# Attention over 16 heads: v and k^T v computed as G = x^T k and G Wv, with the gate's bias carried by a constant column of x

## The reference

```python
h = einsum('bhid,oi,od->bho', x, weighted_sum, weight)     # x (4,512,256,4)
h = concatenate([h, txt], axis=1)                          # (4,1024,256)
n = layernorm(h)                                           # no scale, no shift
q = elu(n @ Wq) + 1;  k = elu(n @ Wk) + 1                  # W* (256,1024): 16 heads of 64
v = n @ Wv;           g = sigmoid(n @ Wg + bg)
kv = einsum('bhnd,bhne->bhde', k, v);  k_sum = k.sum(axis=-2)
z = 1 / clip(einsum('bhnd,bhd->bhn', q, k_sum), 1e-6)
out = einsum('bhnd,bhde->bhne', q * 64**-0.5, kv) * z * g
h = h + out @ Wo
h = h + ffn(layernorm(h))                                  # two layers, not touched
```

## Time and profile before

| | us |
|---|---|
| median of 3 runs | 2147.8 (2147.47 to 2151.69) |
| the profiled execution | 2146.89 |
| its span, first to last instruction | 2145.1 |
| PE busy | 1979.4 (92%) |
| DVE busy | 1547.7 (72%) |
| ACT busy | 1088.3 (51%) |
| POOL busy | 435.6 (20%) |
| mean granted clock of PE | 0.969 |

### The profile page before, as it was taken

One profiled execution on the slowest core, in us unless ns is written; L12 is line 12 of the kernel. 1 busy time (PEld: TensorE's weight loads), 2 busy tenths in 40 slices (PEclk: granted clock), 3 DMA queues, 4 the chain that ended last, 5 costly groups with the idle time before them and its releaser, 6 DMA issues. The chain is left out here.

```text
span 2145.1 us, 42708 instructions
## 1 busy us (share of the span) xinstructions
PE 1979.4 (92%) x13792; PEld 1692.4 (79%) x13792; DVE 1547.7 (72%) x4590; ACT 1088.3 (51%) x2517; POOL 435.6 (20%) x265
## 2 busy tenths in 40 slices
PE   8799999899999959999999879995999999959998
PEld 8688788788878847888888668884888888857887
DVE  7356546546636668999998677775899999957777
ACT  5322232232222228888888624443777777743433
POOL 3100000000000014444444200002444444420010
PEclk9899999999999979999999989997999999989999
DMA  8000000000000020000000010001000000000002
GB/s 300 1 1 1 2 1 1 2 1 1 1 2 1 1 105 5 5 5 5 5 5 5 5 61 11 15 5 65 6 5 5 5 5 5 5 16 15 11 10 83
DMA packets 43179, 42.20 MB, mean 20 GB/s; under 512 B 8552, under 2 KB 37959, under 8 KB 43080
## 3 DMA queue, kind: packets, MB, share of 16 engines
q1 hardware_dynamic: 43080, 40.90, 5.8%
HBM read 32.49 MB, written 8.39 MB: 19 GB/s over the span
## 5 line engine op out<-in xcount | busy, mean ns | idle before, releaser
L908 ACT ACTIVATE l_probs<-l_probs,l_negmax 128x256 f32<-128x256 f32 x512 | 253.2, 496 | 65.1 <-DVE l_negmax L989 65.1
L116 PE MATMUL ps<-local_w_hi,l_xT 128*128 128x512 f32 x384 | 167.9, 437 | 37.1 <-DVE l_xT L982 31.2
L862 POOL TENSOR_TENSOR l_t<-l_t,l_t 128x1024 f32<-128x1024 f32 x64 | 152.9, 2388 | 196.3 <-DVE l_t L1035 196.3
L116 PE MATMUL ps<-attn_w_hi,attn_xT_hi 128*128 128x512 f32 x392 | 169.3, 432 | 18.5 <-issue 10.0
L866 POOL TENSOR_TENSOR l_t<-l_t,l_rnorm 128x1024 f32<-128x1024 f32 x64 | 121.9, 1905 | 307.9 <-DVE l_rnorm L1006 307.9
L419 ACT ACTIVATE attn_exp<-ps 128x512 f32<-128x512 f32 x130 | 77.6, 598 | 209.9 <-PE ps L118 209.9
L914 ACT ACTIVATE l_probsT<-ps 128x512 f32<-128x512 f32 x256 | 138.3, 594 | 49.5 <-PE ps L1133 49.5
L117 PE MATMUL ps<-attn_w_lo,attn_xT_hi 128*128 128x512 f32 x392 | 158.5, 404 | 0.0
L118 PE MATMUL ps<-attn_w_hi,attn_xT_lo 128*128 128x512 f32 x392 | 158.0, 403 | 0.0
L510 DVE TENSOR_SCALAR attn_exp<-attn_exp 128x512 f32<-128x512 f32 x130 | 58.8, 453 | 136.6 <-ACT attn_exp L419 136.5
L118 PE MATMUL ps<-local_w_hi,l_xT 128*128 128x512 f32 x384 | 155.4, 405 | 0.0
(11 more groups left out here) (210 smaller groups left out, 5832.2 us busy)
## 6 DMA issues: line engine op xcount, KB each, us to landing
tok_x<-x SPq DMA_DIRECT2D x16, 512.0 KB, 5.6
m_shifted<-shifted SPq DMA_DIRECT2D x20, 256.0 KB, 2.7
shifted<-x SPq DMA_DIRECT2D x64, 64.0 KB, 1.5
out<-x SPq DMA_DIRECT2D x8, 512.0 KB, 4.4
ffn_w_raw<-ffn_w SPq DMA_DIRECT2D x6, 640.0 KB
local_w_raw<-ffn_wqkv SPq DMA_DIRECT2D x4, 768.0 KB, 5.3
h<-txt SPq DMA_DIRECT2D x4, 512.0 KB, 9.6
attn_w_raw<-attn_Wk SPq DMA_DIRECT2D x1, 1024.0 KB, 7.5
```

Source lines behind the costliest of these rows:

```text
L116: nc.tensor.matmul(out, wh, mh, start=start, stop=False, skip_group_check=True)
L862: nc.gpsimd.tensor_tensor(t1[:], t1[:], t2[:], ALU.add).then_inc(s.summed.sem, 1)
L908: last = nc.scalar.activation(v, v, ACT.Exp, bias=nb[:, h:h + 1], scale=-1.0, accum_out=rsum[:, h:h + 1])
```

## The change

- **G in place of v.** kv = k^T v = k^T (x Wv) = (x^T k)^T Wv. In the key stage PE computes G = x^T k (256 x 1024, banks 2 to 5, summed over the tiles of a batch) instead of v; both sides are split, so these are 12 matmuls of 512 columns a tile. ACT splits off k's high part (`key_high`), DVE its low part (`key_low`), likewise for the normalised x as it stands (`xnh`, `xnl`). Once a batch ACT copies G to SBUF (`take_g`, 4 copies) and PE computes G Wv in f32 (`kv_products`, 16 pairs of instructions, moving Wv with a column of zeros or ones).
- **Constant column.** One column of x, number 128, is redundant, since the normalised columns sum to zero: row 128 of every weight is subtracted from all other rows on the chip (`load_base`, `subtract_base`: two more broadcast loads of 512 KB and two POOL subtractions a weight), and the column holds 1. The row that is freed carries the gate's bias, zero for the others. The bias matmuls, their rows and the DVE steps for them are gone. `normalise` becomes two instructions.
- **Where weights are made.** Only Wk is split, and only Wk and Wv shifted, in the token mixer. Wq, Wg (shift on POOL, high part on ACT, low part on POOL) and Wo are done in the key stage of batch 0.
- **Batches.** Batch 0 and batch 3 are written out, `Fori(1, B - 1)` covers 1 and 2. The first batch transposes its tiles between the keys. The last two tiles of a batch pass through the output product during the next batch's key stage; the last batch does without a next one and ends with them alone. `norm.finish` moves from the end of the key stage into u = 0, behind the copies of k^T v.

```diff
             for n in range(JT * B):
                 if n + 2 < JT * B:
                     x_hi(n + 2)
...
                 take(n)
+                if n in (5, 6):
+                    K.high_part(act, s, 0, n - 5)
...
         def _(pool):
-            nc.gpsimd.memset(K.zrow[:], 0.0).then_inc(s.zeroed.sem, 1)
-            nc.gpsimd.memset(ones[:], 1.0)
-            nc.gpsimd.memset(vs[:, :, :, P:VC], 1.0)
+            K.subtract_base(pool, s, 2)
+            K.low_part(pool, s, 2)
+            nc.gpsimd.tensor_copy(wv[:, 1, :, P:VC], K.ident[:, 0:1].unsqueeze(1).to_broadcast([P, PAIRS, 1]))
             nc.gpsimd.memset(kv[:], 0.0).then_inc(s.attn_set.sem, 1)
+            K.subtract_base(pool, s, 3)
+            K.low_part(pool, s, 3)
             pool.wait_ge(*s.attn_wo_hi.after(1))
             nc.gpsimd.tensor_tensor(wol[:], woraw[:], f32(woh[:]), ALU.subtract).then_inc(s.attn_wo_lo.sem, 1)
...
+            def take_g(b):
+
+                act.wait_ge(*s.attn_g_mm.after(TB * b + TB))
+                for half in range(2):
+                    for c in range(KC):
+                        nc.scalar.activation(gt[:, c, half * HALF:(half + 1) * HALF], ps[:, 2 + 2 * c + half],
+                                             ACT.Copy).then_inc(s.attn_gt.sem, 1)
...
+                for j in range(TB):
+                    key_features(b, j)
+                    if first:
+                        if j + 2 < TB:
+                            low(b, j + 2)
+                        if j + 3 < TB:
+                            normalise(b, j + 3)
...
+                    key_low(b, j)
...
-            def kv_products(b, j):
-                pe.wait_ge(*s.attn_feat.after(AB * b + 2 * j + 2))
-                pe.wait_ge(*s.attn_b_done.after(AB * b + 2 * j + 2))
+            def g_products(b, j):
+                pe.wait_ge(*s.attn_klo.after(2 * TB * b + 2 * j + 2))
+                if j == 0:
+                    pe.wait_ge(*s.attn_b_done.after(GB * b))
+                    pe.wait_ge(*s.attn_o.after(OB * b))
+                for c in range(KC):
+                    x = slice(c * P, (c + 1) * P)
+                    for half in range(2):
+                        cols = slice(half * HALF, (half + 1) * HALF)
+                        last = matmul3(nc, ps[:, 2 + 2 * c + half], xnh[:, j, x], xnl[:, j, x],
+                                       kh[:, j % 2, cols], kl[:, j % 2, cols], j == 0, j == TB - 1)
+                last.then_inc(s.attn_g_mm.sem, 1)
+
+            def kv_products(b):
+                pe.wait_ge(*s.attn_gt.after(4 * b + 4))
                 for g, (m0, m1) in enumerate(GROUPS):
                     for m in range(m0, m1):
...
+                        for c in range(KC):
+                            last = nc.tensor.matmul(ps[:, KV_BANKS[g], (m - m0) * VC:(m - m0 + 1) * VC],
+                                                    gt[:, c, m * P:(m + 1) * P], wv[:, c, m, :],
+                                                    start=(c == 0), stop=(c == KC - 1))
...
                 for j in range(TB):
+                    if first and j + 2 < TB:
+                        xt(b, j + 2)
+                    if not first and j == 1:
+                        out_transposes(b - 1, False, STAGES, 1)
+                    if not first and j in (2, 3):
+                        xt(b, j + 4)
                     if j < TB - 1:
                         keys(b, j + 1)
...
+                    if not first and j < 2:
+                        out_products(b - 1, False, STAGES, j)
+                    g_products(b, j)
...
+        def subtract_base(pool, s, k):
+            pool.wait_ge(*s.attn_w[k % 2].after(16 * KC * (k // 2 + 1)))
+            pool.wait_ge(*s.base_in.after(32 * (k + 1) + 16))
+            for c in range(KC):
+                raw = K.attn_raw[k][0][c]
+                row = K.attn_base[:, c].rearrange("p (m n) -> p m n", n=P) if k == 1 else K.attn_base[:, c]
+                last = nc.gpsimd.tensor_tensor(raw, raw, row, ALU.subtract)
+            last.then_inc(s.based.sem, 1)
```

More of the change, by code:

```diff
@@ L528, in residual, with h_stats @@
                                         ALU.add).then_inc(s.attn_t_done.sem, 1)
+            def h_stats(b, last, u):
+                dve.wait_ge(*s.attn_t_done.after(fills(b, last)[0](u, 5) + 1))
+                for w in range(2):
+                    tile = bass.ds(TB * b + 2 * u - 2 + w, 1)
+                    nc.vector.bn_stats(K.h_stats[:, tile], H[:, tile])
             def gated(b, n, *groups):
@@ L614, in _, with xt @@
+            STEADY = 2 * TB + 1 + 4 * STAGES + STATS_STEPS + 3 * len(GROUPS) * TB
+            batches(dve, counting)
+            for which in range(2):
+                ot_lo(B - 1, True, STAGES, which)
+                residual(B - 1, True, STAGES, which)
+            h_stats(B - 1, True, STAGES)
         @block.tensor
         def _(pe):
-            def xt(bank, xn_n, slot, fill_n):
-                pe.wait_ge(*s.attn_xn.after(xn_n + 1))
-                pe.wait_ge(*s.attn_t_done.room(fill_n, 2))
+            def xt(b, j):
+                n = xt_fill(b, j)
+                pe.wait_ge(*s.attn_xn.after(TB * b + j + 1))
+                pe.wait_ge(*s.attn_t_done.room(n, 2))
@@ L619, in xt, with rows @@
                 for c in range(KC):
-                    last = nc.tensor.transpose(ps[:, bank, c * P:(c + 1) * P], xn[:, slot, c * P:(c + 1) * P], K.ident[:])
+                    last = nc.tensor.transpose(ps[:, 6 + j % 2, c * P:(c + 1) * P], xn[:, j % 2, c * P:(c + 1) * P],
+                                               K.ident[:])
                 last.then_inc(s.attn_t_full.sem, 1)
-            def rows(w, tile, bank0, full, free, count, bias, halves=(0, 1)):
+            def rows(w, tile, bank0, full, free, count, halves=(0, 1)):
@@ L706, in _, with batch @@
-            pe.wait_ge(*s.attn_set.after(1))
-            with pe.Fori(0, B) as b:
-                for j in range(TB):
+                done.then_inc(s.attn_t_full.sem, 1)
+            def batch(b, first, last):
+                if first:
+                    xt(b, 0)
+                    xt(b, 1)
+                keys(b, 0)
+                if not first:
+                    out_transposes(b - 1, False, STAGES, 0)
+                for j in range(TB):
+                    if first and j + 2 < TB:
+                        xt(b, j + 2)
+                    if not first and j == 1:
+                        out_transposes(b - 1, False, STAGES, 1)
+                    if not first and j in (2, 3):
+                        xt(b, j + 4)
```

564 lines of the change are left out of this document (305 added, 259 removed).

## The result

| | before | after |
|---|---|---|
| median of the timed runs, us | 2148.8 (2147.47 to 2151.69) | 2126.0 (2122.05 to 2127.21) |
| the profiled execution / its span | 2146.89 / 2145.1 | 2122.05 / 2120.3 |
| PE busy, DVE busy, POOL busy | 1979.4, 1547.7, 435.6 | 1900.5, 1589.2, 449.2 |
| ratio, 95% interval | | 0.9889 (0.9872 to 0.9906) |

By the ratio the change saves 24 us, 1.1% (22.8 between the medians). The forecast was 2073.6 with a range of 2050 to 2092: the sign was right, two thirds of the gain were missing, and the range did not hold the time.

What follows compares the result with a forecast made beforehand. The prediction took PE's instruction list plus PE's waits to bound the attention. Its terms for mixer and attention summed to 691.2 against 765.4, -74.2 us, giving 2073.6 with a range of 2050 to 2092.

Steps and rivals of the forecast that it cites:

- DMA: 1 MB more ahead of x tiles 2 and 3: Token mixer: the added loads come ahead of x tiles that were 2 us early, later ones 10; no cost summed.
- DVE's steps in the mixer: Token mixer: layernorm steps of tile 9 get stuck beside POOL, tile 10 is 4.5 us late; bounds 0 and 7.
- Batch 0's keys: Batch 0's key stage: DVE stands behind POOL's instructions; first query after 74 us, bounds 54 and 80.
- Bias: Query stages: dropping the bias matmuls saves 0.48 us each, 7.7 a batch, bounds 5 to 8.
- Start of the query stage: Query stage: late norm.finish delays the first gating; 3.0 us of idle PE against 2.05, bounds 2 and 5.
- Key stages of batches 1 to 3: Keys, G, moved output products, transposes and waits take 54.3 us a batch, bounds 53 and 58.
- rival B: Key stages: the key chain becomes the bound; partly, 2092, chance 0.09; slower than before, over 2148, chance 0.02.
- Jumps: Attention loop: three jumps back become one, costing 5.2 us in idle time and slow matmuls; loop entry and exit cost nothing.
- rival C: Loop entry and exit: written-out code costs as a jump does there, +10.4 us, 2084; chance 0.08.
- End: Attention's end: the last two tiles run alone, 14.5 us with a lower clock, bounds 12.5 and 18.
- Rival A: Batch 0's keys and mixer: PE doesn't pay for DVE standing behind POOL; 20 us less, 2053; chance 0.17.
- Rival D: Key stages: compiled order or reused semaphores serialise G with k; chance 0.02.

Runs made afterwards that it cites:

- e1: The kernel after with the constant column's base row loaded over 128 partitions, not 127, and row 0 zeroed afterwards: 2086.2 us, ratio 0.9704.
- e2: The kernel after with the base rows read from a DRAM array holding all 128 copies, still over 127 partitions: 2130.3 us.
- e3: The kernel before with one extra load over 127 partitions into memory that nothing reads: 2173.3 us.
- e4: The kernel before with one extra load over 128 partitions into memory that nothing reads: 2148.8 us.
- e7: e1 with POOL's work beside batch 0's keys made short, most of Wq's and Wg's shift and three low parts left out: 2072.5 us, ratio 0.9645.
- e9: The kernel before without the 64 bf16 matmuls that add the gate's bias: 2124.6 us, ratio 0.9876.
- e10: The kernel before with k^T v cut to one of 8 pairs for tiles 0 to 6 of a batch: 2112.4 us, ratio 0.9829.
- e5: e1 with norm.finish moved to the end of the key stage: 2082.0 us, ratio 0.9693.
- e12: e1 with norm.finish at the key stage's end, all batches written out and POOL's subtractions in quarters: 2067.9 us, ratio 0.9621.
- e11: e1 with POOL's subtractions beside batch 0's keys in quarters, Wo's in eighths: 2078.7 us, ratio 0.9666.

## Why the prediction was wrong, point by point

The predicted span was 2145.1 - 74.2 = 2070.9, the kernel after has 2120.3, e1 2082.5.

| term | sum | after | e1 |
|---|---|---|---|
| token mixer, to the attention's start | 64.4 | 100.6 (+36.2) | 66.1 (+1.7) |
| batch 0's keys | 74.3 | 73.5 (-0.8) | 70.8 (-3.5) |
| first query of batch 0 to that of batch 3 | 448.0 | 458.8 (+10.8) | 460.2 (+12.2) |
| rest | 1484.2 | 1487.4 (+3.2) | 1485.3 (+1.1) |

- **The step that failed: "DMA: 1 MB more ahead of x tiles 2 and 3, which were 2 us ahead of their use; later tiles are 10 us ahead."** It priced the loads by volume and so put them at nothing. One of the two was a load over 127 partitions, which ran on one engine of 16 with x tiles behind it in the queue, and PE stood 20.7 and 17.1 us. The mixer's term of +4.5, bounds 0 and 7, was +40.7; with 128 partitions (e1) it was +6.2. e1 to e4 show the cause. The diff had the `P - 1`; I read it as 4 KB less. The bound was drawn from what was already in the queue, so it could not hold a load of a kind that the kernel before doesn't have.
- *DVE's steps in the mixer* were right: in e1, without the slow loads, the mixer grew by 6.2 where 4.5 was summed. Two steps of the layernorm's statistics, with 8 and 16 columns, got stuck beside POOL's two subtractions of 39.81 to 44.14, one behind each, and PE waited 3.42 us for a later tile, as walked through from the earlier trace rows. The rest is a stretch at the lower clock behind that wait, and the 1.33 that PE waited because of the loads' volume, for which the sum had nothing. DVE's timeline of e1:

```profile
40.05 1.99 DVE L151 TENSOR_SCALAR attn_mean<-attn_rstd 128x8 f32<-128x8 f32 x1
42.07 2.10 DVE L152 TENSOR_TENSOR attn_dev<-attn_stats,attn_mean 128x16 f32<-128x16 f32 x1
```

- *Batch 0's keys*, 73.5 against 74.3, look like a hit and are half an accident. In the kernel after PE's long stops there (5.95 and 7.96 us) come from the late bases: ACT has the high part of Wq and Wg in its list ahead of the exps, and stood 6.12 and 8.12 us for POOL's shift. With the loads mended (e1) the lock takes over, 70.8 us, and e7 gives its price: 14.6 us (12 to 15 over the kernels with the same code), where the sum had 20 (74.3 - 54). The lower bound, 54 without any of it, measured 56.2. ACT's timeline of the kernel after:

```profile
121.16 2.00 ACT L1796 ACTIVATE attn_w_hi<-attn_w_raw 128x1024 fp32r<-128x1024 f32 x2 [6.12 <-POOL attn_w_raw L1790]
...
149.69 2.00 ACT L1796 ACTIVATE attn_w_hi<-attn_w_raw 128x1024 fp32r<-128x1024 f32 x2 [8.12 <-POOL attn_w_raw L1790]
```

- *Bias*, 7.7 a batch: 6.7 by e9, for three waits for the gating took its place in part; the kernel after has them too, 0.46 us each. *k^T v*, 3.4 a batch behind the keys: 3.49 (176.97 to 180.46); e10 agrees with the saving.
- *Start of the query stage*: the late `norm.finish` was summed at 1.0; e5 says 2.1, and 3.8 or more where the clock falls. The waits came as 1.71 and 0.91 us for gating, in order as described. A further 1.4 us a batch, not in the sum, are longer waits for `attn_qT` (1.30 and 1.29 for 0.65 and 0.55 before). The prediction put x's low parts into the room of the key stages; from batch 1 on six of a batch's eight are made in the query stage before it, ahead of a feature that PE waits for. With 1.0 of the bias, 1.1 of finish and these 1.4, the 3.3 us a batch beyond the sum (150.9 for 147.6) are about accounted for.
- *Key stages of batches 1 to 3*, 54.3: 54.6. The new chain never became the bound; rival B is out.
- *Jumps*: one stop (3.35 us, at 425.31) where there were three, 5.2 summed; e5, with the loop, against e12, without it, makes it 4.0 (152.8 to 148.8). No stop without a releaser stands where written-out code goes into the loop or leaves it, in any of the kernels, so rival C is out, too.
- *End*: 90 + 14.5 summed, 105.4 measured. PE's first wait there was 3.40, the second 1.41.
- Rival A (the lock isn't paid) is out by e7. Rival D (G serialised with k) is out by the key stages of 54.6 above.
- *The range*: it holds e1's 2086, the kernel without the slow loads. There the terms that were worked out from rows missed by 12 us together: the stretch between the first queries of batch 0 and batch 3 by +12.2, the others by little in sum. The 36 us came from an operation that was not seen to be of a new kind. Every rival was about engines and none about a queue.

## What to carry to other kernels

For every DMA that a change adds, look at its partition count before its bytes (127 went to one engine): load all 128 partitions and overwrite the odd one afterwards. A slow transfer is paid by what stands behind it, here the x tiles, so PE's wait names DVE, three steps away from the cause: follow the releasers to the end and then read the windows' DMA share. Where POOL has to work beside a DVE chain on PE's path, short POOL instructions cost less than long ones, though their sum is greater (here 61.3 and 62.1 us of a stage for 68.0 to 70.9). And work taken from PE's list comes back in part as waits for the engine behind it: ask for each stage which engine has room, not for the kernel.

## What the runs showed of the hardware that was not expected

- One load over 127 partitions (508 KB) ran at 23 to 29 GB/s, with 0.06 to 0.07 of the DMA engines busy, whether its source was one repeated row or dense; with loads over 128 in its place, the queue moved 370 to 380 GB/s.
- A late gating of 2.02 us, in the middle of busy work, was followed by PE at 0.50 of its clock for some 3 us, which cost some 1.7 us more (152.74 against 150.77, less the 0.28 by which the wait was longer); one of 1.74 was not. In the kernel after, one wait of 2.01 us (at 497.14) was followed by it and another (at 342.08) was not, so the length of the wait alone doesn't decide it.
- DVE beside a POOL subtraction: a step of 8 columns took 1.99 us in place of 0.17, and a minimum 4.33 in place of 0.42, each until POOL's instruction ended. Half a us in which of the two engines starts first moved one stage by 3 us between kernels with the same code there (70.8 and 70.9, 68.0 and 68.0). The Trainium skill, SBUF — State Buffer, § Who interferes with whom, calls it an exclusive lock; e11 agrees that it is taken per instruction.
